# Second attention: TensorE's pieces in halves on neighbouring heads, and a 512-column matmul of zeros before every second head's scores

## What is computed

```python
def _L0_attn_ref(x, W_qkv, W_out, b_out):
    ...
    q8, q_scale = act_quant(q)          # x / (max|x| / 448), rounded to e4m3
    k8, k_scale = act_quant(k)
    scores = jnp.einsum('bhqd,bhkd->bhqk', q8.astype(jnp.float32), k8.astype(jnp.float32))
    scores = scores * (q_scale * k_scale) / jnp.sqrt(jnp.float32(hd))
    attn = jax.nn.softmax(scores, axis=-1)
    v8, v_scale = act_quant(v)
    out = jnp.einsum('bhqk,bhkd->bhqd', attn, v8.astype(jnp.float32))
    out = out * v_scale
    out = out.transpose(0, 2, 1, 3).reshape(B, S, H)
    return jnp.einsum('bsh,ho->bso', out, W_out) + b_out
```

## Time and profile before

| | |
|---|---|
| median of three runs | 1082.24 us (1080.93 to 1088.04) |
| the profiled execution's own time | 1084.97 us |
| its span, first to last instruction | 1083.2 us |
| mean granted clock of TensorE over the span | 0.945 of full |
| PE, PEld busy | 79 %, 50 % |
| DVE, ACT, POOL busy | 62 %, 46 %, 36 % |
| second attention, from the first `scores` to the first matmul of the next stage | 205.7 to 315.0 us |

### The profile page before, as it was taken

How to read it: one execution, slowest core, us unless ns; L and a number is a source line. 1 busy time by engine, 2 the same in 40 slices (tenths; PEclk the granted TensorE clock), 3 DMA queues, 4 the chain that set the end, 5 groups by cost and what they waited for, 6 DMA issues and landing times.

```text
span 1083.2 us, 39645 instructions
## 1 busy us (share of the span) xinstructions
PE 855.8 (79%) x16359; PEld 544.3 (50%) x16359; DVE 674.9 (62%) x2314; ACT 494.8 (46%) x1987; POOL 391.7 (36%) x473
## 2 busy tenths in 40 slices
PE   3778777788989786969688796967766899999717
PEld 3444443344545464546455464645444567667506
DVE  5644544756434576676667676666766567667573
ACT  2423333456531465656565465655555435435201
POOL 0476550454316294674829285670020000000000
PEclk9999999959899898999999899999999899999768
DMA  8000000400000000000000000000200000000101
GB/s 258 6 1 1 2 1 1 145 2 2 1 20 8 6 6 11 4 14 4 14 4 13 4 4 13 5 14 4 51 34 4 2 1 0 0 0 0 40 0 39
DMA packets 32519, 20.00 MB, mean 18 GB/s; under 512 B 23136, under 2 KB 29280, under 8 KB 32352
## 3 DMA queue, kind: packets, MB, share of 16 engines
q1 hardware_dynamic: 27168, 17.04, 5.6%
q10 hardware_dynamic: 5184, 0.59, 0.4%
HBM read 14.47 MB, written 1.05 MB: 14 GB/s over the span
## 4 chain that ended last, share of the span: by engine, by line
PE 59%; DVE 23%; ACT 7%; issue 6%; POOL 0%; DMA 0%; ACTq 0%; DVEq 0%; POOLq 0%
PE banks L1378 15%; PE banks L1325 5%; PE banks L322 4%; DVE work L1661 4%; DVE gate_r L1657 4%; DVE h_ring L1675 3%; PE banks L1348 3%; ACT nzh L1507 3%; DVE pre_n L1666 3%; PE banks L1690 3%; PE banks L307 3%; PE banks L336 2%; PE banks L551 2%; PE banks L523 2%; PE banks L975 2%
## 5 line engine op out<-in xcount | busy, mean ns | idle before, releaser
L1378 PE MATMUL banks<-w_qkv,h_ring 128*4 128x64 f32 x12288 | 228.1, 223 | 111.0 <-DVE h_ring L1675 98.2
L1378 PEld LDWEIGHTS banks<-w_qkv,h_ring 128*4 128x4 f32 x12288 | 178.5, 89 | 214.4 <-DVE h_ring L1675 197.2
L1498 ACT ACTIVATE banks<-gate_r 128x8 f32<-128x8 f32 x256 | 46.2, 180 | 182.0 <-DVE gate_r L1657 182.0
L307 PE MATMUL banks<-zero 128*128 128x512 bf16 x360 | 113.0, 395 | 2.0 <-PE banks L461 2.0
L1657 DVE STREAM_TRANSPOSE gate_r<-banks 128x64 f32<-128x64 f32 x256 | 64.0, 250 | 79.3 <-PE banks L1378 75.5
L1661 DVE STREAM_TRANSPOSE work<-banks 128x64 f32<-128x64 f32 x256 | 76.6, 299 | 2.9 <-PE banks L1378 2.6
L1675 DVE TENSOR_TENSOR_SCAN h_ring<-banks,nzh 128x24 f32<-128x24 f32 x256 | 52.9, 207 | 32.4 <-ACT nzh L1507 0.8
L1666 DVE TENSOR_TENSOR_SCAN pre_n<-banks,work 128x16 f32<-128x16 f32 x256 | 48.7, 190 | 26.9 <-DVE work L1661 0.9
L1668 DVE STREAM_TRANSPOSE banks<-gate_z 128x64 f32<-128x64 f32 x256 | 60.4, 236 | 6.0 <-ACT gate_z L1503 4.8
L1532 POOL TENSOR_TENSOR work<-work 128x512 f32<-128x512 f32 x14 | 17.8, 1271 | 125.1 <-ACT work L1435 125.1
L1503 ACT ACTIVATE gate_z<-banks 128x64 f32<-128x64 f32 x256 | 57.1, 223 | 11.0 <-PE banks L1378 10.6
(11 more groups left out here) (394 smaller groups left out, 1820.2 us busy)
## 6 DMA issues: line engine op xcount, KB each, us to landing
big<-in_x SPq DMA_DIRECT2D x1, 1024.0 KB, 5.8
w_gate<-in_L_ffn_w_gate SPq DMA_DIRECT2D x1, 1024.0 KB, 5.0
shared<-in_L_ffn_w_down SPq DMA_DIRECT2D x1, 1024.0 KB, 7.6
w_gate<-in_L_ffn_W SPq DMA_DIRECT2D x1, 1024.0 KB, 7.0
shared<-in_L_ffn_W SPq DMA_DIRECT2D x1, 1024.0 KB, 6.6
out_x<-big SPq DMA_DIRECT2D x4, 256.0 KB, 2.2
w_qkv<-in_L_cond_W_qkv SPq DMA_DIRECT2D x1, 768.0 KB, 7.0
w_qkv<-in_L_attn_W_qkv SPq DMA_DIRECT2D x1, 768.0 KB, 8.7
```

The lines of the kernel that those rows point to most:

```text
L307: nc.tensor.matmul(bank[:, :], zero16[:, 0:P], zero16[:, :], start=True, stop=True, skip_group_check=True)
L1378: mm = nc.tensor.matmul(bank[32 * j:32 * j + B, 0:64], h_col(t, c), w_hh[:, c, g, :].rearrange("p (m n) -> p m n", m=KC)[:, :, 32 * j:32 * ...
```

## The change

1. **Zeros.** `scores` has one matmul of zeros ahead of every head with odd H, all through the stage. Of the first eight heads, the first four keep two, and the next four have one each.
2. **Halves.** `values`, `projected` and `resample` are cut in two: `values` at h mod 4 = 1 and 2, `projected` at h = 11 and 12 instead of 9, `resample` at h = 7 and 8 instead of 12.
3. **Places and banks.** `heads_in` goes to h = 0 and 3 instead of 0 and 2, and its second side to pY; `out_rows` to 5 and 7 instead of 3 and 5; `out_cols` to 9 instead of 7. `resample` goes to pY and lags two batches instead of one, so that one of the four leaves the loop and runs after the last `values`. ACT's and DVE's partners of each piece move with it (DVE's `exponents` from h = 2 and 8 to 1 and 11), and the waits on pX and pY are new to fit.
4. **POOL.** In batch 0 `split` of the second group comes ahead of `rounded_v(0)` and of `pushed(1, 2, 3)`, and `rounded_v(1)` goes behind the fourth `split`.
5. **End.** The three zeros after the last `values` give way to `resample(2)`; three zeros are added after `out_cols`.

The diff, cut to its core:

```diff
             def heads_in(b, side):
-                pe.wait_ge(p_qk, b + 1)
-                if side and b:
-                    pe.wait_ge(p_tc, 2 * b + 1)
-                elif b >= 3:
-                    pe.wait_ge(e_xgc, b - 2)
-                out = pR if side and b == 0 else pX
+                out = (pR if b == 0 else pY) if side else pX
+                if side == 0:
+                    pe.wait_ge(p_qk, b + 1)
+                    if b >= 3:
+                        pe.wait_ge(p_x, b - 2)
+                elif b:
+                    pe.wait_ge(a_re, Q + 4 * b - 2)
...
-                keep_warm(2 if H < LEAD else 0, bank[H % 3])
+                if H < LEAD or H % 2:
+                    keep_warm(2 if H < 4 else 1, bank[H % 3])
...
             def rows_again(G):
...
+                if g == 2 and b + 1 < B:
+                    pe.wait_ge(p_tc, 2 * b + 4)
+                if g == 3 and b >= 2:
+                    pe.wait_ge(e_xgc, b - 1)
...
+            def resample(b, out, m):
+                if m == 0:
+                    pe.wait_ge(e_gm, b + 1)
+                    pe.wait_ge(p_x, b + 1)
+                    if b + 2 < B:
+                        pe.wait_ge(a_re, Q + 4 * b + 11)
...
-                if H % 4 == 1 and H > 4:
-                    values(H // 4 - 1)
-                if b >= 0 and b + 1 < B and h in (0, 2):
-                    heads_in(b + 1, h // 2)
-                if b >= 1 and h in (3, 5):
-                    out_rows(b - 1, (h - 3) // 2)
-                if b >= 1 and h == 7:
+                if H % 4 in (1, 2) and H > 4:
+                    values(H // 4 - 1, H % 4 - 1)
+                if b >= 0 and b + 1 < B and h in (0, 3):
+                    heads_in(b + 1, h // 3)
+                if b >= 1 and h in (5, 7):
+                    out_rows(b - 1, (h - 5) // 2)
+                if b >= 2 and h in (7, 8):
+                    resample(b - 2, pY, h - 7)
+                if b >= 1 and h == 9:
                     out_cols(b - 1)
-                if b >= 1 and h == 9:
-                    projected(b - 1)
-                if b >= 1 and h == 12:
-                    resample(b - 1, pX)
-            values(4 * B - 1)
-            keep_warm(3, bank[1])
+                if b >= 1 and h in (11, 12):
+                    projected(b - 1, h - 11)
+            for t in range(ST):
+                values(4 * B - 1, t)
+            for m in range(KC):
+                resample(B - 2, bank[3], m)
             for t in range(ST):
                 out_rows(B - 1, t)
             keep_warm(3, bank[1])
             out_cols(B - 1)
-            projected(B - 1)
+            keep_warm(3, bank[1])
+            for m in range(KC):
+                projected(B - 1, m)
...
         def phase2_pool(pool):
...
                 split(4 * b)
                 if b == 0:
                     pushed(0, 2, 3)
-                    rounded_v(0)
-                if b + 1 < B:
+                elif b + 1 < B:
                     pushed(b + 1, 2, 3)
                 split(4 * b + 1)
-                if b + 1 < B:
+                if b == 0:
+                    rounded_v(0)
+                    pushed(1, 2, 3)
+                elif b + 1 < B:
                     rounded_v(b + 1)
```

More of the change, by code:

```diff
@@ L964, in by_key, with values @@
                 mm.then_inc(a_k, 1)
-            def values(G):
+            def values(G, t):
                 b, g = divmod(G, 4)
[L968 to L977, removed]
+                if t == 0:
+                    pe.wait_ge(a_exp, Q + 4 * G + 4)
+                    if g == 0:
+                        pe.wait_ge(p_v8, b + 1)
+                    if g % 2 == 0 and G:
+                        pe.wait_ge(a_oqc, 2 * B + G // 2)
+                for j in range(4):
+                    mm = nc.tensor.matmul(pR[32 * j:32 * j + 32, (g % 2) * S:(g % 2 + 1) * S], vs[b % 2][:, t, 4 * g + j, :],
+                                          prob[(4 * G + j) % 8][:, t * S:(t + 1) * S], start=(t == 0), stop=(t == ST - 1), skip_group_check=True)
+                if t == ST - 1:
+                    mm.then_inc(a_v, 1)
             def out_rows(b, t):
@@ L982, in out_rows @@
                     if b + 2 < B:
-                        pe.wait_ge(p_tc, 2 * b + 6)
+                        pe.wait_ge(p_tc, 2 * b + 5)
                     else:
-                        pe.wait_ge(e_xgc, b)
+                        pe.wait_ge(p_x, b)
                 elif b + 1 < B:
@@ L998, in out_cols, with projected @@
                 mm.then_inc(a_ot, 1)
[L1000 to L1015, removed]
+            def resample(b, out, m):
[4 more added lines that the diff above has]
+                        pe.wait_ge(a_re, Q + 4 * b + 11)
+                for k in range(KC):
+                    mm = nc.tensor.matmul(out[:, m * S:(m + 1) * S], gmats[b][:, k, m * P:(m + 1) * P], xT[:, k, b * S:(b + 1) * S],
+                                          start=(k == 0), stop=(k == KC - 1), skip_group_check=True)
+                if m == KC - 1:
+                    mm.then_inc(e_xg, 1)
+            def projected(b, m):
+                if m == 0:
+                    pe.wait_ge(a_otc, B + b + 1)
+                for k in range(KC):
+                    mm = nc.tensor.matmul(pX[:, m * S:(m + 1) * S], w_out2[:, k, m * P:(m + 1) * P], oT[:, k, :],
+                                          start=(k == 0), stop=(k == KC - 1), skip_group_check=True)
+                if m == KC - 1:
+                    mm.then_inc(p_proj, 1)
             pe.wait_ge(s_am, 1)
@@ L1051, in phase2_pe @@
             out_cols(B - 1)
-            projected(B - 1)
+            keep_warm(3, bank[1])
+            for m in range(KC):
+                projected(B - 1, m)
             keep_warm(6, bank[1])
-            resample(B - 1, pY)
+            for m in range(KC):
+                resample(B - 1, pY, m)
             pe.wait_ge(e_xg, B)
@@ L1061, in heads_out @@
                 act.wait_ge(p_t, 2 * b + side + 1)
-                nc.scalar.copy((qT16s, kT16s)[side][b % 2].rearrange("p g s -> p (g s)"), pX.bitcast(BF16)).then_inc(p_tc, 1)
+                nc.scalar.copy((qT16s, kT16s)[side][b % 2].rearrange("p g s -> p (g s)"), (pX, pY)[side].bitcast(BF16)).then_inc(p_tc, 1)
             def out_of_groups(b, n):
@@ L1176, in phase2_pool @@
                 split(4 * b + 3)
+                if b == 0:
+                    rounded_v(1)
                 if b + 2 < B:
```

27 lines of the change are left out of this document (14 added, 13 removed).

## The result

The changed kernel took 1131.1 us (median of four executions, 1116.95 to 1131.95), the kernel before 1085.1 us beside it (1080.93 to 1091.15): a ratio of 1.039, 95 % interval 1.029 to 1.049. The forecast was 1082 with a range of 1074 to 1092. The ratios leave out executions more than 1.5 % above the fastest of their kernel, and for `e0` and `e5`, whose executions lie too far apart for that, the single times are given.

A forecast was written before the change was run, and what follows sets the result against it. PE's sequence of work, priced by its clock, was taken to bound the stage. Terms +3.0 - 2.4 + 0.1 - 1.5 + 1.2 = +0.4 gave 1085.4 us, or 1079.4 with an earlier clock return; forecast the middle, 1082, range 1074 to 1092.

The forecast's parts named there:

- What bounds the kernel: In the changed stage, ACT and DVE wait for PE; PE's own sequence sets the pace, and depends on its clock.
- The start and POOL: Ahead of batch 0: PE's 2.28 us wait for POOL goes, a 1.7 us wait for DVE's copy comes; gain taken as 0.
- Batch 0, +3.0 at half clock: Four groups at 6.2 us instead of 5.49 add 2.8 us, the start 0.2, with the clock as low as before.
- To return somewhere between the middle of batch 0 ... and the first heads of batch 1: Full clock expected back between batch 0's halves of values beside zeros and batch 1's heads_in: 1079.4 to 1085.4 us.
- Batches 1 to 3, -2.4, +0.1, -1.5: Us per batch: less half clock and shorter PE waits, against added zeros, lost neighbours and breaks; batch 1 also loses one resample.
- Zeros at the full clock, +2.2 for columns and +1.5 for neighbours: In batch 1 or 2, eight zeros at 0.27 us, and three heads no longer beside a neighbour at 0.51 us each.
- End, +1.2: After the last values, resample(2) at 1.90 us replaces 0.75 us of zeros; zeros after out_cols cost nothing under ACT's copy.
- Rival 2: Half clock lasts into batch 1, to the halves of projected at h = 11: +7.2, 1092.6, up to 1097 us; chance 0.15.
- Rival 1: Full clock holds or returns with the first group; batch 0 takes 17.2 us: 1075.8, 1070 to 1078 around it; chance 0.17.
- The rules of the two pages: Tiling mode changes drain the engine, already inside 0.27 and 0.53 us; sustained matmul activity returns the clock, 21.96 busy us against it.

The follow-up runs named there:

- e0: The changed kernel as it is, timed again in a later session: 1090.8, 1124.5, 1109.0 and 1087.7 us.
- e5: The changed kernel with two zeros ahead of each of heads 4 to 7, three ahead of 8 to 11: 1129.6, 1129.0, 1136.4 and 1110.2 us.
- e1: The changed kernel without the zeros ahead of every second head after the first eight, pieces still halved: 1109.9 us, 1.019 of the kernel before.
- e8: The changed kernel with all pieces whole and no zeros ahead of every second head, places and banks as changed: 1084.6 us, 0.997 of the kernel before.
- e3: The changed kernel with values, projected and resample whole again, zeros, places and banks as changed: 1098.5 us, 1.009 of the kernel before.
- e9: The changed kernel with values alone whole again, zeros as changed: 1100.1 us, 1.011 of the kernel before.
- e10: The changed kernel with projected and resample whole again, values halved, zeros as changed: 1103.7 us, 1.015 of the kernel before.
- e12: The changed kernel with whole pieces, more early zeros, eight zeros ahead of heads 12 and 24, no other later zeros: 1088.7 us, 1.002 of the kernel before.
- e14: The changed kernel with whole pieces, more early zeros, eight ahead of heads 12 and 24, pairs where H mod 4 = 3: 1086.4 us, 0.996 of the kernel before.
- e13: The changed kernel with whole pieces, more early zeros, eight ahead of heads 12 and 24, one ahead of later odd heads: 1091.7 us, 1.003 of the kernel before.
- e6: The kernel before with three matmuls of zeros ahead of the scores of heads 8 to 11: 1088.2 us, 0.994 of the kernel before.
- e4: The changed kernel with ten zeros in place of one ahead of head 25, early in batch 1: 1092.2 us, 1.002 of the kernel before.

## Why the prediction was wrong

- **What bounds the kernel:** right. PE's sequence sets the pace and its clock the price. ACT and DVE wait.
- **The start and POOL:** right on the waits. The wait for the second `split` went, and one of 1.31 us for `rows_out` took its place (1.7 forecast). The clock fell near the start and a little earlier, as forecast, but ahead of that wait and not behind it.
- **Batch 0, +3.0 at half clock:** +3.5, though here the clock was low from 0.9 us into the batch and before from 3.7 us. The zero at half clock costs 0.54 (0.49 taken), a group 6.32 us (6.2).
- **"To return somewhere between the middle of batch 0 ... and the first heads of batch 1":** this is the step that failed. In the profiled execution it returned at 338.3, in batch 3. The forecast asked only what the zeros add to each group, and not what the halving takes away. `e1` and `e8` differ by the halving alone, and by 51 us of half clock; `e3`, `e9` and `e10` give one or all whole pieces back and end the half clock in batch 1. The batches at half clock took 37.0 and 40.6 us, where 22.4 and 22.9 were forecast. That it may return where the forecast had it is shown by one profile of `e0`, but of eight executions only two were as fast as that.
- **Batches 1 to 3, -2.4, +0.1, -1.5:** sizes right for a case that seldom came. In that profile of `e0` the batches take 21.4, 22.7 and 19.1 us; the forecast's sums are 24.8 - 2.4 = 22.4, 22.8 + 0.1 = 22.9 and 20.3 - 1.5 = 18.8.
- **Zeros at the full clock, +2.2 for columns and +1.5 for neighbours:** the parts were mis-sized against each other. Measured are 0.5 and 1.6 (`e12` to `e14`), together 2.1 where 3.7 was booked. Part of the columns lies in waits that I booked apart.
- **End, +1.2:** +1.0.
- **Rival 2** named the mechanism, a half clock that lasts because the zeros don't lift PE's work enough, and its sign. It ended it at the halves of `projected` at h = 11 of batch 1 and so priced it at 1092.6 to 1097. The halves of `projected`, with a head between, did not end it; the whole one in `e10` did. The cap was too low: six of the eight executions lie above 1108.
- **Rival 1** had 17.2 us for batch 0 at full clock. `e13` and `e14` stood at the full clock there with the changed places and whole pieces and took 22.4 and 21.9, but each has two bursts of eight zeros in that batch. In `e14` they take 219.10 to 220.92 and 232.86 to 234.69, 3.65 us in all, which leaves 18.3 as an estimate, with early zeros in it that the change doesn't have. So 17.2 is neither refuted nor shown, and 1075.8 for the whole was not tested.
- **The rules of the two pages.** The Trainium skill, "TensorEngine Tiling (Array Packing)" (Tiling Modes, Key Properties), has a change of tiling mode drain the array. That agrees with the 2.1 against 0.5 us of `e13` and `e14`, though these don't part the drain from the lost overlap. The Trainium skill, "TensorE: Matmul & The Clock Gate" (Part 1), has sustained matmul activity bring the clock back. On this stage it did not: PE was busy for 114.28 of 119.5 us at 0.50.

## What to carry to other kernels

When a stage runs at a lowered clock, look in the trace for the long piece behind which the clock comes back, and don't split or spread that piece for the sake of an even rhythm. Price a rearrangement at both clock levels, and read the profiles of several executions, since one kernel took 1088 or 1132 us by where its clock came back. Zeros that keep an engine warm belong where it waits or next to other work on the whole array, not between two small matmuls that would run side by side.

## What the runs showed of the hardware

PE can be busy 96 % of the time for 119.5 us at half clock without getting the full one, with work on 32 of 128 rows and short pieces on all rows taking turns. In other profiles the full clock came back behind longer unbroken work on all rows: a whole `values` with the piece after it, 2.7 to 2.9 us (`e3`, `e6`, `e9`, `e12`), a whole `projected`, 3.7 us (`e10`), `heads_in` and a part of the burst (`e4`).

Length alone is not the whole of it. In `e8` pieces of 2.9 and 3.7 us went by at half clock, and in batch 2 of the changed kernel `out_rows` and half a `resample` stood together from 296.91 to 299.66, 2.75 us, without effect. In `e0` the clock came back behind no more than `heads_in`, 1.0 us, with half a `values`, a matmul of zeros and two heads ahead of it. What else decides was not tried, and the eight executions of one kernel, 1088 to 1132 us, show that it is not the program alone.
